# Cross-attention with sparsemax and a mixture of experts: scores in four row tiles of 32 partitions instead of two of 64

## The reference

```python
x = x + xattn(layernorm(x), ctx, ctx)      # 16 heads of 16 features, bias on q, k, v, out
#   scores = einsum('bhqd,bhkd->bhqk', qh, kh) * 16 ** -0.5
#   attn   = sparsemax(scores)             # clip(scores - tau, 0), rows sum to 1
#   out    = einsum('bhqk,bhkd->bhqd', attn, vh) @ Wo + bo
x = x + ffn(layernorm(x))                  # 8 experts, the best 2 by gate logits + bias,
#   weights sigmoid of the logits, normalised; hidden = relu(x @ w1.T) ** 2; plus one shared expert
```

## Time and profile before

| | |
|---|---|
| median of 3 runs | 917.6 us (917.48 to 919.5) |
| profiled execution | 916.7 us, span 914.9 us |
| TensorE busy | 801.5 us, 88% |
| VectorE, ScalarE, GpSimd busy | 65%, 62%, 59% |
| mean granted TensorE clock | 0.957 |
| score matmuls L739 | 320 instructions |

### The profile page before, as it was taken

How to read it: one execution, slowest core, us unless ns; L and a number is a source line. 1 busy time by engine, 2 the same in 40 slices (tenths; PEclk the granted TensorE clock), 3 DMA queues, 4 the chain that set the end, 5 groups by cost and what they waited for, 6 DMA issues and landing times.

```text
span 914.9 us, 14519 instructions
## 1 busy us (share of the span) xinstructions
PE 801.5 (88%) x4800; PEld 656.7 (72%) x4800; DVE 593.5 (65%) x1691; ACT 571.3 (62%) x890; POOL 538.3 (59%) x622
## 2 busy tenths in 40 slices
PE   1847657999999999999999999999999999889998
PEld 1535435778777777878777877777787877767887
DVE  2469685867676867768586777786777858642221
ACT  1555667676668676767767666867676776633221
POOL 2447586766667584848686666768484858541010
PEclk9977577999999999999999999999999999989999
DMA  8300101020200202020102020110202010101010
GB/s 253 103 8 1 19 12 47 1 73 6 69 3 25 53 12 59 12 64 14 59 1 72 7 70 1 35 43 12 59 13 64 3 59 1 59 1 59 1 58 11
DMA packets 37355, 34.84 MB, mean 38 GB/s; under 512 B 23153, under 2 KB 34078, under 8 KB 35230
## 3 DMA queue, kind: packets, MB, share of 16 engines
q1 hardware_dynamic: 34934, 28.88, 11.3%
q0 software_dynamic: 1248, 4.73, 1.5%
q10 hardware_dynamic: 1096, 0.29, 0.2%
HBM read 28.30 MB, written 4.33 MB: 36 GB/s over the span
## 4 chain that ended last, share of the span: by engine, by line
PE 45%; ACT 22%; issue 15%; DVE 9%; POOL 5%; DMA 3%; ACTq 0%; POOLq 0%; DVEq 0%
PE y_ps L827 18%; PE h_ps L814 11%; ACT signs L533 10%; ACT hid L584 5%; PE m_ps L778 5%; ACT over L535 4%; PE s_ps L769 4%; POOL over L337 3%; DVE fsum L955 3%; PE m_ps L722 3%; DMA sw_all<-sw_scratch 2%; DVE fold_b L961 2%; ACT xn L481 1%; DVE g L1080 1%; PE m_ps L803 1%
## 5 line engine op out<-in xcount | busy, mean ns | idle before, releaser
L337 POOL TENSOR_TENSOR over<-S,tau 128x1232 f32<-128x1232 f32 x128 | 286.6, 2251 | 232.7 <-DVE tau L973 230.1
L827 PE MATMUL y_ps<-w_sb,hid 128*128 128x256 f32 x1152 | 281.5, 388 | 39.9 <-ACT hid L584 30.2
L814 PE MATMUL h_ps<-x1nT,w_sb 128*128 128x256 f32 x1152 | 275.6, 382 | 0.0
L827 PEld LDWEIGHTS y_ps<-w_sb,hid 128*128 128x128 f32 x1152 | 212.8, 191 | 86.1 <-ACT hid L584 57.7
L814 PEld LDWEIGHTS h_ps<-x1nT,w_sb 128*128 128x128 f32 x1152 | 215.2, 191 | 30.4 <-issue 3.0
L955 DVE TENSOR_REDUCE fsum<-over 128x16 f32<-128x1232 f32 x96 | 137.4, 1431 | 40.7 <-ACT over L535 40.6
L535 ACT ACTIVATE over<-over 128x1232 f32<-128x1232 f32 x128 | 155.6, 1228 | 3.0
L584 ACT ACTIVATE hid<-g 128x512 f32<-128x512 f32 x144 | 89.6, 622 | 65.2 <-DVE g L1080 64.7
L1080 DVE SCALAR_TENSOR_TENSOR g<-h_ps,sw_all 128x512 f32<-128x512 f32 x128 | 87.5, 684 | 58.0 <-PE h_ps L814 36.8
L533 ACT ACTIVATE signs<-over 128x1232 bf16<-128x1232 f32 x96 | 117.1, 1220 | 7.4 <-POOL over L337 7.2
L952 DVE TENSOR_TENSOR fold_a<-signs 128x640 bf16<-128x640 bf16 x96 | 55.7, 580 | 47.2 <-ACT signs L533 47.2
(11 more groups left out here) (104 smaller groups left out, 922.4 us busy)
## 6 DMA issues: line engine op xcount, KB each, us to landing
sw_all<-sw_scratch SPq DMA_DIRECT2D x16, 1024.0 KB, 5.2
x_sb<-in_x SPq DMA_DIRECT2D x16, 256.0 KB, 2.7
w_sb<-in_w POOLq DMA_DIRECT2D x2, 2048.0 KB, 12.1
out_y<-wk_sb SPq DMA_DIRECT2D x16, 256.0 KB, 5.6
sw_all<-in_ctx SPq DMA_DIRECT2D x1, 1078.0 KB
v_block<-v_all SPq DMA_DIRECT2D x56, 9.6 KB
wk_sb<-in_wk SPq DMA_DIRECT2D x1, 256.0 KB
wv_sb<-in_wv SPq DMA_DIRECT2D x1, 256.0 KB
```

Source lines behind the costliest of these rows:

```text
L337: return pool.tensor_tensor(dst, S[:, p, t], tau[:, p, t].rearrange("p (h o) -> p h o", o=1).broadcast_to([P, NH, NK]), ALU.subtract)
L814: last = pe.matmul(h_ps[:, i % 2, c, :], w1_sb[:, e, k, c * P:(c + 1) * P], x1nT[:, p, k, :], start=(k == 0), stop=(k == KC - 1))
L827: last = pe.matmul(y_ps[:, t, :], hid[:, i % 2, c, t * P:(t + 1) * P], w2_sb[:, e, c, :], start=(i == 0 and t == 0 and c == 0), stop=(i == ...
```

## The change

A group of the block-diagonal layout becomes 32 partitions with two heads. `k_diag` is 2 x 77 columns wide, and the mask that makes it is repeated four times over the partitions instead of twice. `new_scores` on TensorE issues eight matmuls of 154 columns for each token tile, four row tiles for c = 0 and four for c = 1. Row tiles 0 to 2 write banks 0 to 2 of `s_ps`, row tile 3 writes bank 0 of `m_ps`; each bank gets 2 x 154 columns, all from one row tile, and the wait on `s_front` and its semaphore go. ScalarE's first eviction takes the three banks of `s_ps`, its second the bank of `m_ps`, and both write S in the order of the model's heads: places 8c + 2r + j. With that PLACES goes, and the product's column tile and half follow from the pair's number alone.

```diff
--- before.py
+++ after.py
@@ -27,9 +27,10 @@
 SPARE = 18
 BANK = 512
 SB = 3
-HALF = P // 2
-GH = HALF // DH
-PLACES = (0, 1, 2, 3, 14, 15, 4, 5, 6, 7, 12, 13, 8, 9, 10, 11)
+ROWS = 32
+RT = P // ROWS
+GH = ROWS // DH
+HALF_KEYS = GH * NK
 FLAT = NH * NK
 CHUNKS = -(-FLAT // P)
 LAST = FLAT - (CHUNKS - 1) * P
@@ -177,7 +178,7 @@
         swT_done, swT_taken = sig("swT_done"), sig("swT_taken")
 
         k_diag_ready = sig("k_diag_ready")
-        s_front, s_done, s_taken = sig("s_front", T), sig("s_done", T), sig("s_taken", T)
+        s_done, s_taken = sig("s_done", T), sig("s_taken", T)
         veps_ready, rstd_ready, shift_ready = sig("veps_ready", T), sig("rstd_ready"), sig("shift_ready")
         xn_ready = sig("xn_ready", T)
         ln_chain = sig("ln_chain", 2 * T)
@@ -267,7 +268,7 @@
                 for c, s, lo, hi in PIECES:
                     sp.dma_start(v_block[lo - c * P:hi - c * P, ring:ring + 2, BLOCKS.index((c, s // 2)),
                                          s % 2 * DH:(s % 2 + 1) * DH],
-                                 v_all[lo - s * NK:hi - s * NK, 2 * i:2 * i + 2, PLACES[s] * DH:(PLACES[s] + 1) * DH]
+                                 v_all[lo - s * NK:hi - s * NK, 2 * i:2 * i + 2, s * DH:(s + 1) * DH]
                                  ).then_inc(v_placed[i % 2], 16)
 
             def turn(b, p, q, new=False, late=False, old=False):
@@ -517,11 +518,11 @@
             def new_scores(b, p, t):
                 act.wait_ge(s_done.sem, s_done.at(b, t + 1))
                 act.wait_ge(attn_checked.sem, attn_checked.at(b - 2))
-                flat = S[:, p, t].rearrange("p h k -> p (h k)")
-                act.activation(flat[:, 0:12 * NK].rearrange("p (a n) -> p a n", a=2), s_ps[:, 0:2, 0:6 * NK],
+                slots = S[:, p, t].rearrange("p (c r j) k -> p r c (j k)", c=KC, j=GH)
+                act.activation(slots[:, 0:SB], s_ps[:, :, 0:KC * HALF_KEYS].rearrange("p r (c n) -> p r c n", c=KC),
                                ACT.Copy, scale=DH ** -0.5)
-                act.activation(flat[:, 12 * NK:], s_ps[:, 2, 0:4 * NK], ACT.Copy, scale=DH ** -0.5
-                               ).then_inc(s_taken.sem, 1)
+                act.activation(slots[:, SB], m_ps[:, 0, 0:KC * HALF_KEYS].rearrange("p (c n) -> p c n", c=KC),
+                               ACT.Copy, scale=DH ** -0.5).then_inc(s_taken.sem, 1)
 
             def sign_relu(b, p, r, t):
                 act.wait_ge(over_ready.sem, over_ready.at(b, rt(r, t)))
@@ -731,16 +732,12 @@
                 else:
                     pe.wait_ge(aT_taken.sem, aT_taken.at(b - 3))
 
-                for c, r, h0, n, bank, col in ((0, 0, 0, 4, 0, 0), (0, 1, 0, 4, 1, 0), (1, 0, 0, 4, 2, 0),
-                                               (1, 1, 2, 2, 0, 4), (1, 1, 0, 2, 1, 4)):
-                    rows = slice(r * HALF, (r + 1) * HALF)
-                    if (c, bank) == (1, 0):
-                        pe.wait_ge(s_front.sem, s_front.at(b, t + 1))
-                    last = pe.matmul(s_ps[:, bank, col * NK:(col + n) * NK], qT[rows, c, t * P:(t + 1) * P],
-                                     k_diag[rows, c, h0:h0 + n, :].rearrange("p h k -> p (h k)"),
-                                     start=True, stop=True)
-                    if (c, bank) == (0, 0):
-                        last.then_inc(s_front.sem, 1)
+                for c in range(KC):
+                    for r in range(RT):
+                        rows = slice(r * ROWS, (r + 1) * ROWS)
+                        bank = s_ps[:, r] if r < SB else m_ps[:, 0]
+                        last = pe.matmul(bank[:, c * HALF_KEYS:(c + 1) * HALF_KEYS], qT[rows, c, t * P:(t + 1) * P],
+                                         k_diag[rows, c].rearrange("p h k -> p (h k)"), start=True, stop=True)
                 last.then_inc(s_done.sem, 1)
 
             def late_unsettled(m):
@@ -772,8 +769,7 @@
                     pe.wait_ge(aT_taken.sem, aT_taken.at(m, SB * t + i + 1))
                     for c, a in blocks:
                         rows = min(P, FLAT - c * P)
-                        pair = PLACES[2 * a] // 2
-                        half, quad = pair // 4, pair % 4
+                        half, quad = a // RT, a % RT
                         order = [k for bank in BY_BANK for k, o in bank if o == a]
                         last = pe.matmul(m_ps[32 * quad:32 * quad + 32, t, half * P:(half + 1) * P],
                                          v_block[0:rows, m % RING, BLOCKS.index((c, a)), :], attnT[0:rows, c, :],
@@ -1165,7 +1161,7 @@
         "cfc": turned(a["cfc"]), "cproj": turned(a["cproj"]),
 
         "ident": np.eye(P, dtype=np.float32),
-        "head_of": np.tile(np.repeat(np.eye(GH, dtype=np.float32), DH, axis=0), (2, 1)),
+        "head_of": np.tile(np.repeat(np.eye(GH, dtype=np.float32), DH, axis=0), (RT, 1)),
         "iota": np.tile(np.arange(E, dtype=np.float32), (P, 1)),
     }
     nc = bacc.Bacc("TRN2", target_bir_lowering=False, num_devices=1)
```

## The result

The changed kernel takes 930.88 us (median, 929.95 to 932.88), the kernel before 917.54 beside it: ratio 1.0155, 95% interval 1.0115 to 1.0195. It is slower by 13 us. A second measurement, of six executions, gave 928.89 against 917.77, ratio 1.0096 (1.0067 to 1.0126); one of the six, at 938.8 us, is over 1.5% above the fastest and is left out of that ratio. The ratios are those on record and are not quotients of the medians, which would be 1.0145 and 1.012. The forecast was 916.0, with a range up to 919.8, so it was wrong. The profiled execution took 930.64 us, span 928.7.

The account below looks back on a forecast made before the run. TensorE is 88% busy, but two tied chains of waits without score groups hold a steady turn: 0 there, 1.3 + 0 + 0.3 = 1.6 us in the first three turns, so a median of 916.0 us, range 911.5 to 919.8.

Parts of the forecast that it names:

- The score group: Score matmuls on TensorE: four row tiles run side by side, a group takes 0.78 us against 1.63.
- The other estimate: Score matmuls: 0.68 us for a group's streaming, from the Trainium skill's 3.07 times speed for four row tiles.
- The waits: Steady turn, TensorE: wait ahead of the second score group grows 0.15 to 1.00 us, behind it 0.29 to about 1.1.
- The evictions, the keys, the product: Evictions same time, larger 0.92 us; key block about 0.6 instead of 1.22 us, worth 0; product 0, +-1.5 us in all.
- The cover of 1.1 us: Second score group may start 1.1 us late before `hid` is missed; even 1.2 us more on the first pair costs nothing.
- A steady turn at full clock: From the fourth turn on: a turn still takes 49.4 us after the change.
- the tie of the two chains: Steady turn: TensorE's own path and the chain through GpSimd and ScalarE's norm reach TensorE's turning (L795) almost together.
- The first turns: First three turns, scores on the path: gains of 1.3, 0 and 0.3 us, 1.6 in all.
- the pricing of a steady turn: 13 steady turns: worth 0 each, 22 us of TensorE time turn into wait; bounds +-1.3 us.
- The rival on the clock: First turns: half-clock stretches lost or won; one lost 917.7 us, two won 912.6; chance 0.05 for a loss within the bound.
- The rival of 931 us: Score matmuls: row tiles take turns, a group takes 2.24 us, layer 2 starts 0.78 late each steady turn; chance 0.06.

Follow-up runs that it names:

- e0: The changed kernel itself, measured again with no edit: 928.89 us.
- e5: The changed kernel with VectorE's gating product of expert 2 put between the two sums of Newton round 2: 906.3 us, ratio 0.9866.
- e6: The kernel before with VectorE's gating product of expert 2 put between the two sums of Newton round 2: 907.13 us, ratio 0.9895.
- e1: The changed kernel with the score group of token tile 1 issued twice over the same values: 917.28 us, ratio 1.001.
- e2: The changed kernel with half of layer 1 of expert 3 issued twice, ahead of the second score group: 917.84 us, ratio 0.9999.
- e3: The kernel before with expert 3's layer 1 cut to 2 of 8 instructions and expert 1's layer 2 to 4 of 8: 931.97 us, ratio 1.0176.
- e4: The changed kernel with two query matmuls (0.87 us) issued once more in a single turn, that of example 8: 938.97 us, ratio 1.0253.

## Why the prediction was wrong, point by point

*The score group.* Forecast 0.78 us, measured 0.81. Four row tiles do run side by side, which the trace before could not show: the first instructions of all four start between 402.05 and 402.07. Right. The other estimate, 0.68 us for the streaming alone, was too high: less the prediction's 0.10 and 0.16 for the first load and the tail, 0.81 leaves 0.55.

*The waits.* Forecast 1.00 and 1.1, measured 0.97 and 1.08. The second group's release by the eviction and the layer-2 group's by `hid` held to 0.02 us. Right.

*The evictions, the keys, the product.* The first eviction 0.924 against 0.922 us; the product's instructions 284 ns against 282; nothing came of either. (The cover of 1.1 us could not have held 1.2 us on the first pair, as the prediction says; with the eviction unchanged it was not needed.) Of the keys only the size was off: forecast 0.6, measured 0.704,

```profile
L325 POOL TENSOR_TENSOR k_diag<-kT,head_of x16: 700/704/951, 22.6 to 750.5; 128x308 f32<-128x308 f32 x16
```

and it cost or gave nothing.

*A steady turn at full clock.* Forecast 49.4, measured 49.40 in four turns of the first trace and in six of e0. Right, and so was the tie of the two chains, which e5 and e6 show from either side.

*The first turns.* Forecast 1.6 us gained, measured 2.3 to the fourth example's scores. The second example's scores start at 61.33 instead of 62.46, 1.1 earlier where I had 1.3. The rest of the gain comes in the second turn (41.51 us instead of 42.57), for which I took 0, and almost nothing in the third (50.37 instead of 50.44), for which I took 0.3. Since these turns differ by more than 3 us between traces of the same instructions, neither the gain nor its parts are shown.

*The step that failed* is in the pricing of a steady turn: "Worth: 0 in each of the 13 steady turns; 13 x 2 x 0.85 = 22 us of TensorE time turn into wait." I took a wait that is off the chain to cost nothing, with bounds of +-1.3 us. TensorE's wait isn't free: its clock is granted by what it does, and two waits of about 1 us with 0.81 us of work between them, once a turn, were enough for a fall to half. The rival on the clock was there, and the rows on which it stood, but I kept it to the first turns. Each fall costs 1.80 us, and eight turns with one cost the 14.5 us, eleven times the bound. That the steady part had run at full clock with waits of 0.15 and 0.29 said nothing of waits of 1.0 and 1.1. e1, e2 and e3 show this from three sides: fill either wait and the loss goes; make waits in the kernel before and it comes.

*The rival of 931 us*, tiles that take turns, hit the number by accident. Its mechanism, a group of 2.24 us, is refuted by the 0.81.

*How the loss repeats.* After its first fall the first trace never had a turn of 49.4 again: each has one stretch of 3.41 us at half clock, beginning 7.1 us after the start of its scores. Before, the same waits stood in four turns (in e0: in six) and nothing fell. That is shown. That a turn lengthened to 51.2 us brings the waits back to the same place against the chip's clock changes is how I read it; the 51.20 us between falls in e3 and e4, whatever the turns take, speaks for it, and in e4 the delay moved the waits against that interval by only 0.72 us (7.76 to 7.04), which was too little. But no run broke the repetition by a shift alone. It stays argued. Open too is why e4 began in its second steady turn and cost more in its timed runs (932.6 to 942.3) than in its profile.

## What to carry to other kernels

Time taken off TensorE that becomes wait is not always free: look at where the new waits come to stand, and give a chance to a fall of the granted clock where short waits gather, even if the clock has been full there. A few full-clock turns prove nothing; here the falls began after four in one execution and after six in another. A busy share and clock slices averaged over 23 us hide a fall of 3.4 us; ask for the clock of each stretch, and compare the lengths of single turns. And before making the engine with the most busy time faster, find the small instruction that releases it: moving one gating product of 0.68 us gave about 1%, the 26 us off the score groups nothing that can be measured.

## What had not been expected of the hardware

The granted clock fell to 0.5 for 3.41 us with TensorE busy over 90% of the turn (45.11 of 49.39 us in a turn that takes no fall), behind waits of 0.97 and 1.09 us. In the first trace it recurred in every turn from 357.95 to the end of the scores; in e0 from 455.1. The falls stood 51.20 us apart, in e3 and e4 too, where the turns took 50.93 to 51.92. Filling one of the two waits with 0.5 to 0.9 us of matmuls that change nothing gave 917.3 and 917.8 us, where the changed kernel had 930.9 and 928.9.
